# Cross attention of layer 0: the steps that fill the score tasks are placed from the back, each at its last allowed task

## The reference

```python
x = x + attn(layernorm(x))          # layer 0 self attention
x = x + xattn(layernorm(x), mask, ctx)
...
q, k, v = h @ Wq, h @ Wk, h @ Wv    # 32 heads of 16; rotary on q and k
w  = softmax(q k^T / 4 + mask)      # over the 112 own tokens
aw = tanh(gate) * softmax(q ak^T / 4)   # ak = ctx @ Wk, 375 tokens
out = (w v + aw av) @ Wo            # av = ctx @ Wv
```

## Time and profile before

| | us |
|---|---|
| median of 3 runs | 1882.57 (1880.48 to 1887.6) |
| span of the profiled execution | 1882.7 |
| PE busy | 1809.5 (96%) |
| DVE busy | 999.0 (53%) |
| ACT busy | 606.8 (32%) |
| cross attention tasks, first scores to first step after the last values | 427.41 to 976.37 |

### The profile page before, as it was taken

How to read it: one execution, slowest core, us unless ns; L and a number is a source line. 1 busy time by engine, 2 the same in 40 slices (tenths; PEclk the granted TensorE clock), 3 DMA queues, 4 the chain that set the end, 5 groups by cost and what they waited for, 6 DMA issues and landing times.

```text
span 1882.7 us, 29157 instructions
## 1 busy us (share of the span) xinstructions
PE 1809.5 (96%) x11794; PEld 1192.0 (63%) x11794; DVE 999.0 (53%) x1860; ACT 606.8 (32%) x1931; POOL 386.0 (21%) x456
## 2 busy tenths in 40 slices
PE   7999999999999999999889899999999999999998
PEld 6766666646665666666555788886676674444444
DVE  4755666426656656566644111116654455565887
ACT  1233222315655555555640111111312213232511
POOL 2532323411010110110004000005221130002476
PEclk9999999999999999999888999999999999999999
DMA  9100002000000000000205988865100021643011
GB/s 376 42 1 1 1 1 106 1 15 17 18 18 1 18 17 1 18 17 2 112 2 183 364 337 339 336 257 178 79 1 1 1 88 68 242 166 124 1 39 40
DMA packets 31110, 170.70 MB, mean 91 GB/s; under 512 B 3865, under 2 KB 3865, under 8 KB 17185
## 3 DMA queue, kind: packets, MB, share of 16 engines
q1 hardware_dynamic: 28416, 161.50, 22.7%
q0 software_dynamic: 2560, 7.34, 1.3%
HBM read 155.98 MB, written 16.52 MB: 92 GB/s over the span
## 4 chain that ended last, share of the span: by engine, by line
PE 84%; DVE 9%; POOL 3%; issue 2%; ACT 2%; DMA 1%; POOLq 0%; DVEq 0%; SPq 0%; ACTq 0%
PE PS L1156 8%; PE PS L993 6%; PE PS L1236 6%; PE PS L944 6%; PE PS L1300 5%; PE PS L1033 4%; PE PS L1024 4%; PE PS L1196 4%; PE PS L1165 4%; PE PS L1072 4%; PE PS L1269 3%; PE PS L1056 3%; PE PS L1287 3%; PE PS L1092 2%; PE PS L1001 2%
## 5 line engine op out<-in xcount | busy, mean ns | idle before, releaser
L2063 POOL TENSOR_TENSOR rstd<-veps,mhalf 112x1 f32<-112x1 f32 (+1 forms) x76 | 58.1, 764 | 614.8 <-DVE veps L1329 591.3
L1156 PEld LDWEIGHTS PS<-R,W 128*128 128x128 f32 x1344 | 154.6, 193 | 11.7 <-issue 11.7
L1156 PE MATMUL PS<-R,W 128*128 128x128 f32 x1344 | 155.0, 277 | 2.2 <-DVE R L1627 2.2
L1456 DVE TENSOR_REDUCE nmx<-PS 112x2 f32<-112x750 f32 x128 | 114.1, 933 | 76.8 <-PE PS L1056 76.8
L1927 ACT ACTIVATE R<-PS,nmx 112x375 f32<-112x375 f32 x256 | 143.1, 574 | 3.7 <-DVE nmx L1456 3.7
L944 PE MATMUL PS<-xT,W 128*128 128x224 f32 x640 | 127.1, 359 | 1.0 <-ACT xT L1858 0.7
L944 PEld LDWEIGHTS PS<-xT,W 128*128 128x128 f32 x640 | 122.9, 194 | 7.3 <-issue 5.1
L1634 DVE TENSOR_TENSOR R<-R,PS 128x512 f32<-128x512 f32 x21 | 14.4, 687 | 200.5 <-PE PS L1156 200.5
L1269 PE MATMUL PS<-W 128*128 128x512 f32 x256 | 118.4, 605 | 0.0
L1401 DVE TENSOR_TENSOR x<-x,PS 112x512 f32<-112x512 f32 x40 | 27.5, 688 | 171.2 <-PE PS L993 83.6
L993 PE MATMUL PS<-W,R 128*112 128x512 f32 x256 | 114.7, 602 | 0.0
(11 more groups left out here) (291 smaller groups left out, 3240.3 us busy)
## 6 DMA issues: line engine op xcount, KB each, us to landing
W<-in_we SPq DMA_DIRECT2D x63, 1024.0 KB, 7.7
W<-in_entwT SPq DMA_DIRECT2D x8, 1024.0 KB, 7.0
W<-in_entpw SPq DMA_DIRECT2D x8, 1024.0 KB, 8.7
W<-in_ctxT SPq DMA_DIRECT2D x8, 750.0 KB, 4.2
R<-in_ctxT SPq DMA_DIRECT2D x8, 750.0 KB, 8.0
R<-in_ctx SPq DMA_DIRECT2D x8, 750.0 KB
xs_rows<-in_x SPq DMA_DIRECT2D x3, 1792.0 KB, 38.4
R<-xs_rows SPq DMA_DIRECT2D x21, 256.0 KB, 8.1
```

Of the source, the lines that this page charges most:

```text
L1156: o = e.matmul(PS[:, m, c * 128:(c + 1) * 128], gate_up(j % 3, k, off + c * 128), BT[:, j % 2, k, :], start=k == 0, stop=k == 3)
L1456: e.tensor_reduce(nmx[0:S, par, r:r + 2], PS[0:S, r:r + 2, 0:SC], AX.X, ALU.max, negate=True).then_inc(*up("cmax", (b, c, par, r)))
```

## The change

`cross` no longer hands out fill batch by batch. A new planner `weave` lists all fill of the stage, gives every item the last task that it may stand at, and goes through the list from the back: it starts at the end of the stage and moves down to an earlier task whenever the present one has less room than half of the item. Room is an even share of the planned work (times 1.02, by `GAP`) less what the task's head and tail cost. A `pj` pair and its two `rt` are now one item of four steps in a row, where they had been interleaved one `pj` ahead. The context's steps are ordered ck 0, ck 1, vx, cv 0 to 2, ck 2, ck 3, so the load of the next context waits for ck 3. The six expert rows are spread over tasks 86 to 91. The waits of two loads follow.

```diff
+def weave(gaps):
+    todo = []
+    for u in range(1, NU):
+        todo += [(24 * u + 3 * c - 2, [("pj", u, c, 0), ("pj", u, c, 1), ("rt", u, c, 0), ("rt", u, c, 1)]) for c in range(4)]
+        if u + 1 < NU:
+            bs = (2 * u + 2, 2 * u + 3)
+            todo += [(24 * u + 8, norms(1, bs)), (24 * u + 13, turns(1, bs[:1])), (24 * u + 14, turns(1, bs[1:]))]
+    for b in range(1, NBATCH):
+        n = 12 * b
+        todo += [(n - 1, [("ck", b, 0)]), (n + 1, [("ck", b, 1)]), (n + 1, [("vx", b)])]
+        todo += [(n + 2 + t, [("cv", b, t)]) for t in range(3)] + [(n + 5, [("ck", b, 2)]), (n + 8, [("ck", b, 3)])]
+    todo.sort(key=lambda item: item[0])
+    late = expert_rows(range(6))
+    extra = [0.0] * len(TASKS)
+    for n in range(len(TASKS) - 10, len(TASKS) - 4):
+        extra[n] += sum(cost(s) for s in late) / 6
+    own = [sum(cost(s) for part in gaps[n] for s in part) for n in range(len(TASKS))]
+    fills = [[] for _ in TASKS]
+    whole = sum(own) + sum(extra) + sum(cost(s) for _, steps in todo for s in steps)
+    unit = 1.02 * whole / sum(GAP[t[2]] for t in TASKS)
+    room = [unit * GAP[t[2]] - own[n] - extra[n] for n, t in enumerate(TASKS)]
+    at, next_ct = len(TASKS) - 1, {}
+    for limit, steps in todo[::-1]:
+        spent = sum(cost(s) for s in steps)
+        if steps[0][0] in ("ck", "cv"):
+            limit = min(limit, next_ct.get(steps[0][1] + 1, limit))
+        least = {"vx": 12 * steps[0][1] - 11, "cv": 12 * steps[0][1] - 9, "ck": 12 * steps[0][1] - 12}.get(steps[0][0], 0)
+        at = min(at, limit)
+        while at > least and room[at] < spent / 2:
+            at -= 1
+        at = max(at, least)
+        room[at] -= spent
+        fills[at] = steps + fills[at]
+        if steps[0][0] in ("ck", "cv"):
+            next_ct[steps[0][1]] = at - 2
...
+    fills[last] += [("load", "front", j) for j in (1, 2, 0)]
+    for k, n in enumerate(range(len(TASKS) - 10, len(TASKS) - 4)):
+        fills[n] += late[k * len(late) // 6:(k + 1) * len(late) // 6]
+    return fills
...
+    fills = weave(gaps)
+    for n, (b, c, kind) in enumerate(TASKS):
+        out.append(("xs", b, c) if kind == "own" else ("xc", b, c, kind))
+        head, tail = gaps[n]
+        out += head + fills[n] + tail
...
-                    w.wait_ge(*at("context", ("cv", n - 1, 2)) if n else at("proj", ("kq0", NU - 1, 9)))
+                    w.wait_ge(*(at("context", ("ck", n - 1, 3)) if n > 1 else at("context", ("cv", 0, 2)) if n else at("proj", ("kq0", NU - 1, 9))))
...
-                        w.wait_ge(*at("context", ("cv", 7, 2)))
+                        w.wait_ge(*at("context", ("ck", 7, 3)))
```

More of the change, by code:

```diff
@@ L296 @@
 FRONT = 12
+def weave(gaps):
[33 more added lines that the diff above has]
+            next_ct[steps[0][1]] = at - 2
+    for b in range(2, NBATCH):
+        last = max(n for n, steps in enumerate(fills) for s in steps if s[0] in ("ck", "cv") and s[1] == b - 1)
+        fills[last].append(("load", "ct", b))
+    last = max(n for n, steps in enumerate(fills) for s in steps if s[0] in ("ck", "cv", "vx"))
+    fills[last] += [("load", "front", j) for j in (1, 2, 0)]
+    for k, n in enumerate(range(len(TASKS) - 10, len(TASKS) - 4)):
+        fills[n] += late[k * len(late) // 6:(k + 1) * len(late) // 6]
+    return fills
@@ L299, in cross @@
 def cross():
     out, gaps = [], attendx()
[L302 to L328, removed]
```

## The result

Over 17 runs of each the changed kernel takes 1889.9 us (median; 1885.07 to 1891.61) against 1882.57; the ratio is 1.0032, 95% interval 1.0023 to 1.0041. The ratio comes to 6 us (4.3 to 7.7); the two medians are 7.3 us apart. So it is slower by more than the measurement's uncertainty and by less than 0.5%. The forecast was 1887 us and a change within 0.5%.

A forecast was written before the change was run, and what follows sets the result against it. PE was taken to bound the stage. Work 513.9, idle 30.5, slow clock 4.6 at the end and 4.4 at other holes sum to 553.4 us, giving 1887 us for the whole; range 1873 to 1900.

The forecast's parts named there:

- PE as the bound, and what can be won: Stage: PE bounds batches 0 to 6; work stays 513.9 us, only 23.2 us idle and 12.0 us slow clock winnable.
- The floor of a task: Scores to next scores take at least 5.75 us (kind 0) or 4.55 (kind 1); without fill, 2.65 or 2.25 us idle.
- Where the holes are: Tasks short of fill after packing from the back: the start, 23, 47, 79, 91, 94 and 95, each idling PE.
- The DVE queue ahead of 23 and 47: Row maxima of tasks 23 and 47 queue behind stats and scales on DVE, 1 us more idle each.
- Everyday waits and rt: Small PE waits over the whole stage, 10.0 us, plus 1.5 us for rt right behind their pj.
- Slow clock: Lowered PE clock behind holes: 4.6 us at the end, plus 4.4 us for two of four other holes.
- The sum: Whole stage: work 513.9, idle 30.5, slow clock 4.6 and 4.4, together 553.4 us against 549.0 before.
- No slow clock outside the end: Rival: holes as priced, no slow clock at the other holes, smaller rt waits; 1880 us, chance 0.13.
- The slow clock at every hole: Rival: each of four holes outside the end costs about 5 us of slow clock; 1903 us, chance 0.25.
- The even load: Rival: dense neighbours make empty tasks free, only 94 and 95 idle, 4.9 us; 1862 us, chance 0.09.
- The front and context loads: Later loads cost nothing: front load from task 92, context loads behind ck 3, apart from 1.7 us at the start.

The follow-up runs named there:

- e1: Kernel before, with one cv in each of batches 0 to 6 moved into the own task ahead, leaving seven tasks without fill; 1912.9 us, ratio 1.0151.
- e9: Changed kernel with the two rt of each pj item behind the task's tail instead of ahead of it; 1879.8 us, one run.
- e8: Kernel of e7 with the fill of each fifth task of a batch ahead of xb instead of behind it; 1863.5 us, ratio 0.9883.
- e5: Changed kernel with only the two groups of stats and scales moved from tasks 22 and 46 to 13 and 37; 1887.5 us, one run.
- e6: Kernel before with one more wait on SP, so the front load starts only behind the scores of task 92; 1884.9 us, ratio 1.0000.
- e2: Changed kernel with its empty middle tasks 23, 47 and 79 filled by moving pj items and the steps ahead of them later; 1871.7 us, ratio 0.9942.
- e7: Changed kernel with start and middle holes filled, stats moved, and the last ck and expert-row turns rearranged at the end; 1868.6 us, ratio 0.9919.
- e10: Kernel of e8 with the two rt of each pj item behind the task's tail, as in e9; 1859.5 us, ratio 0.9876.

## Why the prediction was right, and where it was only lucky

- **PE as the bound, and what can be won.** Right that moved fill counts only by the idle time and slow clock that it makes or saves. Wrong that the work stays: it grew by 3.0 us, the largest single part of the +4.3. It held for moved cv (e1: 513.4) and not for an rt that follows its pj closely (e9). Also too strong: that a move within the PE-bound stretch saves nothing. Its everyday waits could be won in part by placing xb and rt further from their producers (e8, e9).
- **The floor of a task.** Right to 0.1 us: 5.75 and 4.55 predicted from two or three tasks of batch 7; 5.74 and 4.66 measured (e1, e5), with holes of 2.64 and 2.14 us. The 2.6 us from own to kind 0 was no floor but work: where those scores waited, they came 1.9 us after (behind task 0) or 3.1 us (behind 18, 30 and others, held by DVE).
- **Where the holes are.** Right: 0 and 1, 23, 47, 79, 91, 94. Their idle times, predicted and measured: start 3.3 and 3.3, 23 and 47 3.2 and 3.2 each, 79 2.65 and 2.65, 91 1.75 and 1.92, 94 2.65 and 2.63. Task 95 showed none instead of 2.25; the sum had taken that off again for the slow clock, together with 1 us at 94 where the full 2.63 us were idle in fact.
- **The DVE queue ahead of 23 and 47.** Priced at 1 us each, shown by e5 to be 1.06 us each.
- **Everyday waits and rt.** Priced at 11.5 us; 25.4 less the 16.9 us of holes leaves 8.5. Too high by 3. In part this is since the rt, priced at 3.6 us of idle time, show 1.8, and another 1.4 us that e9 took out of the work.
- **Slow clock.** Two slow stretches outside the end were taken, three came. Priced in all at 7.8 + 4.4 = 12.2 us, measured 11.6. The parts were off in opposite ways: three of the four holes outside the end cost 1.7 to 3.3 us each, 6.7 in all instead of 4.4, and the end cost 5.0 instead of 7.8.
- **The sum.** 553.4 us predicted, 553.3 measured. This agreement is luck: two terms cancel, work 3.0 us (or 2.4 against my 513.9) too low, idle time 1.9 too high (27.3 with the 3.2 taken off, against 25.4). What was foreseen by its mechanism, that the holes eat up what batch 7 wins, came to +1.3 us in idle time and slow clock, and the other 3.0 us were not foreseen.
- **The rivals.** No slow clock outside the end fell with three of the four holes. The slow clock at every hole came close in frequency (three of four; six of seven in e1) and not in price: with dense work behind, 1.7 to 3.3 us and not 5. That ck, cv or pj follow did not keep the clock up, as the argument against this rival had it. The even load fell with e1. The front and context loads cost nothing, by e6 and since PE shows a wait for in_ctxT at the start alone.
- The 6 us of the runs are more than the 4.3 us of the stage in one profile; the interval, 4.3 to 7.7 us, reaches down to it. I have no sign of another cause.

## What to carry to other kernels

When a fixed chain sets a floor between two points of the bounding engine's list (here scores to scores: 5.74 us behind kind 0, 4.66 behind kind 1), fill has to reach that floor in every interval; an even share of a sum of costs, packed from one end, leaves empty intervals, and each of them costs its whole gap. Compare per interval, floor against work, before a step is moved. Then look at what stands directly behind its producer: putting xb behind the fill brought the ratio from 0.9919 to 0.9883, some 7 us, without moving any fill from one task to another. Putting rt behind the tail took the waits at rt away in the profiles (e9, e10); that it shortens the whole is not shown (one run, and a ratio that overlaps).

## What the runs showed of the hardware

TensorE's clock falls behind a single short gap more often than I had assumed. Over the stages of the twelve profiles, 50 gaps of 1.7 to 3.4 us stood on PE, and behind 40 of them the granted clock was at its lower level (1.2 of 2.4 GHz) within 5 us. No stretch at the lower level stood in these stages without an idle wait just ahead of it or at its start. The same gap in the same program does both: the 2.94 us near 437 us stayed without consequence before and was followed by the lower clock in e1 and e6, which have the same order there. A slow stretch with dense work behind cost 1.7 to 3.3 us, so a hole comes to much more than its gap: in e1, 16.2 us more idle time and 11.8 us of slow clock behind the holes, (16.2 + 11.8) / 7 = 4.0 us for each. Even two small waits shortly after one another at the xb (0.29 us, then 0.65 to 0.71 within 2 us) were followed by one 7 times out of 21: three times in e1, once each in e2, e5, e6 and e7. Here are those of e1 near 517 us, and the clock behind them:

```profile
515.18 1.15 PE L1114 MATMUL PS<-rT,cst 32*128 32x112 f32 x16 [0.29 <-ACT R L1946]
...
517.04 5.39 PE L1039 MATMUL PS<-W 128*125 128x512 f32 x8 [0.71 <-DVE W L1475]
```

```profile
517.10:520.60 3.50, 3.50 (x5) 1.41 (x6) 1.57 (x3) 1.00 (x4) 0.00 (x0) 0.51 0.02 5
```
